# First weight matrix in two halves, squared half by half, and a first projection that begins with its high-times-high products

## The chip, the cores and the metric

The kernel runs on one core of one Trainium2 chip. The time is that of the device, in microseconds (us), for one execution. Five engines run their own instruction streams in parallel and meet at semaphores: TensorE (PE in the profile, its weight loads PEld), VectorE (DVE), ScalarE (ACT), GpSimd (POOL) and SyncE (SP), which here only issues transfers.

## The reference

One transformer-like layer on x of shape (4, 512, 512): a gated recurrent mixer, then a feed-forward part with a Walsh-Hadamard transform.

```python
def mixer(h, Wi, Wf, Wg, Wo, gnorm_w):          # h = layernorm(x)
    i = einsum('bth,dh->btd', h, Wi)
    f = einsum('bth,dh->btd', h, Wf)
    g = einsum('bth,dh->btd', h, Wg)
    gate = sigmoid(f)
    v = silu(i) * (1.0 - gate)
    o = scan over t of  o[t] = gate[t] * o[t-1] + v[t]
    rms = o * rsqrt(mean(o * o) + 1e-5)
    return einsum('btd,hd->bth', rms * gnorm_w * g * sigmoid(g), Wo)

def ffn(z, W1, W2, W3):                         # z = layernorm(x1)
    hidden = fwht(silu(z @ W1.T) * (z @ W3.T))
    return hidden @ W2.T

x1  = x  + layernorm(mixer(layernorm(x), ...))
out = x1 + layernorm(ffn(layernorm(x1), ...))
```

## The kernel before

The four batches b are worked one after the other, overlapped. Each has 4 row tiles t of 128 rows. Every fp32 operand of a product is split into two fp16 parts, high and low, and a product is made of three TensorE passes: high times high (L615), high times low (L616) and low times high (L617), into one PSUM bank.

The order of the work on each engine is written out in tables (PE_ORDER, ACT_ORDER, DVE_ORDER, POOL_ORDER, SP_ORDER). Each engine runs its table from front to back, and each step waits on semaphores for its inputs. A step is named KIND.b.t; on TensorE a number behind a colon is the PSUM bank. The steps at the start of the program are:

- X1.0.t (DVE L1072 to L1080): statistics of row tile t of batch 0. GpSimd then takes the power -1/2 (L1393).
- X2.0.t (DVE L1085): normalises tile t.
- XT.0.t on PE (L667): four 128x128 fp32 transposes of tile t. XT.0.t on ACT (L866) writes the high part to xb, XT.0.t on DVE (L1094) the low part.
- AQ.w.0 on ACT (L877): squares the whole attention matrix w (0 is W_f, 1 W_i, 2 W_g), 2048 elements in each partition. AQ.3.0 does W_o in two parts (L874).
- AN.w.0 on PE (L689): four matmuls of ones by the squares, a sum over partitions. AN.w.0 on DVE (L1100 and six small ones) makes the scale row_s of the matrix from it.
- AT.w.c on ACT (L881) and on DVE (L1115): the high and the low part of column chunk c of matrix w.
- F.0.c, I.0.c, G.0.c on PE: the projections with W_f, W_i and W_g, 12 matmuls of 512 columns each.
- W2N.m.0 on PE (L760): eight products of unit m of the raw second feed-forward weight with itself, which wait for the load of that unit (w2t).

F.0.0 waits for all four high and all four low parts of x, and for the low part of chunk 0 of W_f:

```python
pe.wait_ge(xt_hi, TC * (b + 1))
pe.wait_ge(xt_lo, TC * (b + 1))
...
pe.wait_ge(aw_lo[w], c + 1)          # in project()
```

All loads go through one queue, issued by SyncE in this order: row tile 0, the identity (eye, for the transposes), row tiles 1 to 3, W_f, W_i, W_g, gnorm, W_o; the row tiles of batch 1, each after the transpose of the tile of batch 0 that it replaces; the Hadamard matrix, eight pairs of W_1 and W_3, four units of W_2, and so on.

Of the kernel before, what the change touches and what calls it, by code (L numbers as in the profile page):

```python
# [42 lines left out]
GA.0.4:6 H2.0.1:0 H2.1.0:2 UP.0.4:5 GA.0.5:7 UP.0.5:3 GA.0.6:1 UP.0.6:6 H2.1.1:5 GA.0.7:7 UP.0.7:3 H2.2.0:1
H2.2.1:6 GA.0.8:4 UP.0.8:0 GA.0.9:7 UP.0.9:3 H2.3.0:2 MS.1.0:4 H2.3.1:5 GA.0.10:1 UP.0.10:0 Y.1.0:7 Y.1.1:1
H2.4.0:4 H2.4.1:3 GA.0.11:6 H2.5.0:2 H2.5.1:0 UP.0.11:5 GA.0.12:6 UP.0.12:7 GA.0.13:5 Y.1.2:6 Y.1.3:1 H2.6.0:7
H2.6.1:4 H2.7.0:3 UP.0.13:2 GA.0.14:0 UP.0.14:6 GA.0.15:5 UP.0.15:7 H2.7.1:2 D.0.0 D.0.1 D.0.2 D.0.3 D.0.4 D.0.5
D.0.6 D.0.7 D.0.8 D.0.9 D.0.10 D.0.11 D.0.12 D.0.13 D.0.14 D.0.15 D.0.16 D.0.17 D.0.18 D.0.19 D.0.20 D.0.21
# [37 lines left out]
AQ.0.0 XT.0.0 XT.0.1 XT.0.2 AQ.1.0 XT.0.3 AT.0.0 AT.0.1 AT.0.2 AQ.2.0 AT.0.3 AT.1.0 AT.1.1 AT.1.2 AQ.3.0 F.0.0  # L85
AT.1.3 AT.2.0 AT.2.1 I.0.0 WN.0.0 AT.2.2 XT.1.0 F.0.1 WN.1.0 AT.3.0 G.0.0 WN.2.0 I.0.1 AT.2.3 S.0.0 P.0.0 XT.1.1
F.0.2 XT.1.2 I.0.2 AT.3.1 G.0.1 S.0.1 XT.1.3 AT.3.2 P.0.1 AT.3.3 F.0.3 G.0.2 I.0.3 S.0.2 F.1.0 P.0.2 WN.3.0
S.0.3 G.0.3 P.0.3 F.1.1 I.1.0 G.1.0 WN.4.0 WN.5.0 I.1.1 WN.6.0 WN.7.0 S.1.0 YN.0.0 YN.0.1 YN.0.2 YN.0.3 WT.0.0
WT.0.1 WT.1.0 WT.1.1 ZT.0.0 WT.2.0 F.1.2 P.1.0 F.1.3 WT.2.1 G.1.1 S.1.1 ZT.0.1 ZT.0.2 ZT.0.3 I.1.2 GA.0.0 P.1.1
# [1404 lines left out]
```

## Time and profile before

| | us |
|---|---|
| median of 3 runs (692.3 to 694.3) | 692.82 |
| the profiled execution | 692.09 |
| its span on the core | 690.3 |
| PE busy | 668.9 (97%) |
| DVE busy | 484.3 (70%) |
| ACT busy | 285.4 (41%) |

The span runs from the first to the last instruction that the profile shows; the profiled execution's own time is 1.8 us longer. The idle time of TensorE is in few places: 8.95 us ahead of its first instruction, and the waits that are listed below. The granted clock of TensorE is shown by stretch as PEclk, 1.00 being 2.4 GHz and 0.50 being 1.2 GHz. A busy time of the matmuls is modelled, so the distance between starts is the better measure of their pace.

### The profile page before, as it was taken

Reading aid. Unit: us, or ns where it says so; the run is one execution under the profiler, and the core shown is the slowest. Engines: PE = TensorE matmul, PEld = TensorE weight load, DVE = VectorE, ACT = ScalarE, POOL = GpSimd, SP = SyncE. Lnnn points to the kernel's source line nnn. Section 1 sums busy time; section 2 is a strip of 40 time slices with the busy share of each in tenths; the row PEclk is TensorE's granted clock in tenths of the full one; section 3 lists DMA queues with packets and bytes.
Section 4 is the critical chain, followed back from the end, with each engine's and each line's share of the span. In section 5 each row is a group of like instructions: output and inputs, shape, how many; then the busy total and the mean of one; then the engine's idle time right before and its main releaser. Section 6 shows DMA issues by size and latency. Waiting matters only on the chain.

```text
span 690.3 us, 10939 instructions
## 1 busy us (share of the span) xinstructions
PE 668.9 (97%) x4132; PEld 407.3 (59%) x4132; DVE 484.3 (70%) x837; ACT 285.4 (41%) x466; POOL 266.5 (39%) x228
## 2 busy tenths in 40 slices
PE   3999999999998999999999999999999999999996
PEld 2545454444443454557877675656666777877762
DVE  6998999998988867976757461717478465744544
ACT  5978565764434325633322231452323221412231
POOL 1299479759254211552522211133256120311221
PEclk9999999999999999999999999999999999999999
DMA  8960421333569986385449336203526933432502
GB/s 340 406 237 24 160 77 51 132 97 117 184 218 297 235 241 226 140 335 181 152 155 275 140 64 227 101 21 123 182 93 173 252 126 122 138 129 101 198 1 92
DMA packets 58820, 113.30 MB, mean 164 GB/s; under 512 B 33424, under 2 KB 37776, under 8 KB 54160
## 3 DMA queue, kind: packets, MB, share of 16 engines
...
q8 instruction: 33, 0.54, 0.3%
q14 instruction: 19, 0.16, 0.1%
...
## 4 chain that ended last, share of the span: by engine, by line
PE 90%; DMA 4%; DVE 2%; issue 1%; SPq 1%; POOL 1%; ACT 0%; DVEq 0%; POOLq 0%
PE ps L615 29%; PE ps L616 29%; PE ps L617 29%; DMA w2t<-W2t 2%; PE ps L775 2%; PE ps L667 1%; DMA ring<-W13t 1%; DMA rows<-L_attn_hidden_states 1%; SPq L522 1%; PE ps L726 1%; PE ps L760 0%; POOL rstd L1393 0%; DVE ring L1278 0%; DVE w2t L1342 0%; DVE sg L1168 0%
## 5 line engine op out<-in xcount | busy, mean ns | idle before, releaser
L615 PE MATMUL ps<-xb,ring 128*128 128x256 f16 (+1 forms) x704 | 225.9, 321 | 1.1 <-DVE ring L1115 1.0
L617 PE MATMUL ps<-xb,ring 128*128 128x256 f16 (+1 forms) x704 | 225.9, 321 | 0.0
L616 PE MATMUL ps<-xb,ring 128*128 128x256 f16 (+1 forms) x704 | 225.9, 321 | 0.0
L615 PEld LDWEIGHTS ps<-xb,ring 128*128 128x128 f16 x704 | 69.1, 98 | 48.0 <-issue 3.3
L616 PEld LDWEIGHTS ps<-xb,ring 128*128 128x128 f16 x704 | 68.9, 98 | 46.7 <-issue 2.7
L1393 POOL TENSOR_TENSOR rstd<-var,neg_half 128x1 f32<-128x1 f32 x64 | 46.0, 723 | 125.3 <-DVE var L1080 38.5
L617 PEld LDWEIGHTS ps<-xb,ring 128*128 128x128 f16 x704 | 68.8, 98 | 42.1
L1450 POOL TENSOR_TENSOR ring<-sga,ring 128x512 f16<-128x512 f32 x36 | 47.8, 1334 | 117.3 <-ACT ring L1029 117.3
L616 PE MATMUL ps<-ring 128*128 128x256 f16 x288 | 78.5, 273 | 0.0
L617 PE MATMUL ps<-ring 128*128 128x256 f16 x288 | 78.5, 273 | 0.0
L615 PE MATMUL ps<-ring 128*128 128x256 f16 x288 | 78.5, 273 | 0.0
L1292 DVE TENSOR_TENSOR ring<-ps,junk 128x512 f32<-128x512 f32 x48 | 32.9, 687 | 55.5 <-ACT sga L1017 25.1
L1450 POOL TENSOR_TENSOR hsp<-sga,hsp 128x512 f16<-128x512 f32 x24 | 29.0, 1216 | 82.1 <-ACT hsp L1029 82.1
L1302 DVE TENSOR_TENSOR ring<-ps,ring 128x512 f32<-128x512 f32 x48 | 33.0, 687 | 34.4 <-PE ps L617 33.1
L996 ACT ACTIVATE junk<-ps 128x256 f32<-128x256 f32 x48 | 18.1, 380 | 91.8 <-PE ps L617 87.0
L615 PE MATMUL ps<-w2t,ring 128*128 128x512 f16 x144 | 54.6, 379 | 0.0
L616 PE MATMUL ps<-w2t,ring 128*128 128x512 f16 x144 | 54.6, 379 | 0.0
L617 PE MATMUL ps<-w2t,ring 128*128 128x512 f16 x144 | 54.6, 379 | 0.0
L1313 DVE TENSOR_TENSOR ring<-ps,ring 128x512 f32<-128x512 f32 x48 | 32.8, 686 | 28.8 <-PE ps L617 28.7
L1362 DVE SCALAR_TENSOR_TENSOR sga<-ring,up_c,sga 128x512 f32<-128x512 f32 x48 | 38.2, 808 | 13.3 <-ACT sga L1017 12.9
L1017 ACT ACTIVATE sga<-ring,gate_c 128x512 f32<-128x512 f32 x48 | 33.8, 716 | 29.0 <-DVE ring L1313 11.6
L1029 ACT ACTIVATE ring<-sga 128x512 f16<-128x512 f32 x36 | 22.0, 624 | 46.0 <-DVE sga L1362 28.3
...
## 6 DMA issues: line engine op xcount, KB each, us to landing
...
```

What stands on the lines that cost most here:

```text
L615: pe.matmul(dst, a_hi, b_hi, start=start, stop=False)
L616: pe.matmul(dst, a_hi, b_lo, start=False, stop=False)
L617: return pe.matmul(dst, a_lo, b_hi, start=False, stop=stop)
L996: act.activation(p_copy[:, g % 2], bank("GP", b, g)[:, 256:512], ACT.Copy).then_inc(sp_rdy, 1)
L1017: act.activation(sga[:, c % 2], src, ACT.Silu, scale=gate_c[:]).then_inc(sga_rdy, 1)
L1029: act.activation(hid(b, c, 0), sga[:, c % 2], ACT.Copy).then_inc(hid_hi, 1)
L1292: dve.tensor_tensor(combined(g % 2)[:, 0:512].rearrange("p (o t) -> p o t", o=2), bank("GQ", b, g)[:].rearrange("p (o t) -> p o t", o=2), ...
L1302: dve.tensor_tensor(to[:, 512:1024].rearrange("p (o t) -> p o t", o=2), bank("GR", b, g)[:].rearrange("p (o t) -> p o t", o=2), both, ALU. ...
L1313: dve.tensor_tensor(to[:, 512:1024], bank("GU", b, g)[:], to[:, 512:1024], ALU.add).then_inc(gu_rdy, 1)
L1362: dve.scalar_tensor_tensor(sga[:, c % 2], src, up_c[:], sga[:, c % 2], ALU.mult, ALU.mult).then_inc(hid_rdy, 1)
L1393: pool.tensor_tensor(dst, src, neg_half[:].broadcast_to(src.shape), ALU.pow).then_inc(done, 1)
L1450: pool.tensor_tensor(hid(b, c, 1), sga[:, c % 2], hid(b, c, 0), ALU.subtract).then_inc(hid_lo, 1)
```

## The change

W_f comes in two transfers of 512 KB, one issued behind row tile 0, ahead of the identity, and one behind row tile 1. Each half is squared on its own, AQ.0.0 and AQ.0.1. On ACT, AQ.0.1 stands behind XT.0.0, and AQ.1.0 (the squares of W_i) goes from ahead of XT.0.3 to behind AT.0.0. On PE, AN.0.0 goes ahead of XT.0.3, and waits between its second and third matmul for the second half. On DVE, X1.0.2 goes behind X2.0.1, and AN.0.0 goes from behind XT.0.2 to ahead of XT.0.0. F.0.0 makes the same 12 products in another order, four high times high, four high times low and four low times high, with a wait ahead of each group. The five tables are otherwise what they were; they are laid out anew, so of each only its head is shown.

```diff
 PE_ORDER = """
-XT.0.0:4 XT.0.1:5 XT.0.2:6 XT.0.3:7 AN.0.0:0 AN.1.0:1 F.0.0:2 AN.2.0:3 ...
+XT.0.0:4 XT.0.1:5 XT.0.2:6 AN.0.0:0 XT.0.3:7 AN.1.0:1 F.0.0:2 AN.2.0:3 ...
 ACT_ORDER = """
-AQ.0.0 XT.0.0 XT.0.1 XT.0.2 AQ.1.0 XT.0.3 AT.0.0 AT.0.1 AT.0.2 AQ.2.0 ...
+AQ.0.0 XT.0.0 AQ.0.1 XT.0.1 XT.0.2 XT.0.3 AT.0.0 AQ.1.0 AT.0.1 AT.0.2 AQ.2.0 ...
 DVE_ORDER = """
-X1.0.0 X1.0.1 X1.0.2 X2.0.0 X2.0.1 X1.0.3 X2.0.2 X2.0.3 XT.0.0 XT.0.1 XT.0.2 AN.0.0 XT.0.3 ...
+X1.0.0 X1.0.1 X2.0.0 X2.0.1 X1.0.2 X1.0.3 X2.0.2 X2.0.3 AN.0.0 XT.0.0 XT.0.1 XT.0.2 XT.0.3 ...
...
             load_x(0, 0)
+            sp.dma_start(att_raw(0)[:, 0:2], w_f[:, 0:2]).then_inc(ld_aw[0], 16)
             sp.dma_start(ident[:], eye).then_inc(ld_eye, 16)
             load_x(0, 1)
+            sp.dma_start(att_raw(0)[:, 2:4], w_f[:, 2:4]).then_inc(ld_wf, 16)
             load_x(0, 2)
             load_x(0, 3)
-            load_attention(0, w_f)
...
-                pe.wait_ge(aw_sq, w + 1)
+                pe.wait_ge(aw_sq, 1 if w == 0 else w + 2)
...
                 for k in range(KC):
+                    if w == 0 and k == 2:
+                        pe.wait_ge(aw_sq, 2)
...
             def f(b, c):
+                if b == 0 and c == 0:
+                    wait_bank("F", 0, 0)
+                    pe.wait_ge(xt_hi, TC)
+                    pe.wait_ge(aw_hi[0], 1)
+                    w, dst = att_w(0), bank("F", 0, 0)[:]
+                    for k in range(KC):
+                        pe.matmul(dst, w[:, 0, k, chunk(0)], xb[:, 0, 0, k, :], start=k == 0, stop=False)
+                    pe.wait_ge(xt_lo, TC)
+                    for k in range(KC):
+                        pe.matmul(dst, w[:, 0, k, chunk(0)], xb[:, 0, 1, k, :], start=False, stop=False)
+                    pe.wait_ge(aw_lo[0], 1)
+                    for k in range(KC):
+                        last = pe.matmul(dst, w[:, 1, k, chunk(0)], xb[:, 0, 0, k, :], start=False, stop=k == KC - 1)
+                    last.then_inc(f_mm, 1)
+                    return
...
             def square_attention(w, p):
+                if w == 0:
+                    act.wait_ge(ld_wf if p else ld_aw[0], 16)
+                    half = slice(1024 * p, 1024 * (p + 1))
+                    act.activation(squares[0][:, half], att_raw(0).rearrange("p k d -> p (k d)")[:, half], ACT.Square
+                                   ).then_inc(aw_sq, 1)
+                    return
                 act.wait_ge(ld_aw[w], 16)
```

On TensorE at the start of the program, before: the last transposes of x, the sums of squares of W_f (bank ps0) and W_i (ps1), and the first products of F.0.0 (ps2).

```order
L667 MATMUL ps6<-ident,rows 128x128 [waits x_norm]
L667 MATMUL ps6<-ident,rows 128x128 x3
L667 MATMUL ps7<-ident,rows 128x128 [waits x_norm]
L667 MATMUL ps7<-ident,rows 128x128 x3
L689 MATMUL ps0<-ot,ones16 128x512 [waits ones16_set,aw_sq]
L689 MATMUL ps0<-ot,ones16 128x512 x3
L689 MATMUL ps1<-ot,ones16 128x512 [waits aw_sq]
L689 MATMUL ps1<-ot,ones16 128x512 x3
L615 MATMUL ps2<-xb,ring 128x512 [waits aw_lo0,xt_lo,xt_hi]
```

The same place on TensorE in the changed kernel:

```order
L663 MATMUL ps6<-ident,rows 128x128 x3
L687 MATMUL ps0<-ot,ones16 128x512 [waits ones16_set,aw_sq]
L687 MATMUL ps0<-ot,ones16 128x512
L687 MATMUL ps0<-ot,ones16 128x512 [waits aw_sq]
L687 MATMUL ps0<-ot,ones16 128x512
L663 MATMUL ps7<-ident,rows 128x128 [waits x_norm]
L663 MATMUL ps7<-ident,rows 128x128 x3
L687 MATMUL ps1<-ot,ones16 128x512 [waits aw_sq]
L687 MATMUL ps1<-ot,ones16 128x512 x3
L713 MATMUL ps2<-xb,ring 128x512 [waits aw_hi0,xt_hi]
L713 MATMUL ps2<-xb,ring 128x512 x3
L716 MATMUL ps2<-xb,ring 128x512 [waits xt_lo]
```

The sums of W_f now stand ahead of the transposes of tile 3 (ps7). Those of W_i (ps1) still stand ahead of F.0.0 (ps2).

On ScalarE at the start, before: the squares of W_f, the high parts of tiles 0 to 2, the squares of W_i (the second row with ot and 2048), the high part of tile 3, and the first high parts of W_f.

```order
L877 ACTIVATE ot<-ring 128x2048 [waits ld_aw0]
L866 ACTIVATE xb<-ps4 128x4x128 [waits xt_mm]
L866 ACTIVATE xb<-ps5 128x4x128 [waits xt_mm]
L866 ACTIVATE xb<-ps6 128x4x128 [waits xt_mm]
L877 ACTIVATE ot<-ring 128x2048 [waits ld_aw1]
L866 ACTIVATE xb<-ps7 128x4x128 [waits xt_mm]
L881 ACTIVATE ring<-ring,row_s 128x4x128 [waits aw_srdy] x3
```

The same place on ScalarE in the changed kernel:

```order
L885 ACTIVATE ot<-ring 128x1024 [waits ld_aw0]
L879 ACTIVATE xb<-ps4 128x4x128 [waits xt_mm]
L885 ACTIVATE ot<-ring 128x1024 [waits ld_wf_second]
L879 ACTIVATE xb<-ps5 128x4x128 [waits xt_mm]
L879 ACTIVATE xb<-ps6 128x4x128 [waits xt_mm]
L879 ACTIVATE xb<-ps7 128x4x128 [waits xt_mm]
L900 ACTIVATE ring<-ring,row_s 128x4x128 [waits aw_srdy]
L896 ACTIVATE ot<-ring 128x2048 [waits ld_aw1]
L900 ACTIVATE ring<-ring,row_s 128x4x128 [waits aw_srdy] x2
```

The squares of W_i (L896, ot, 2048) now stand behind the high part of tile 3 and behind the first high part of W_f.

## Rows read from the trace of the kernel before

**Rows 1.** Waits of TensorE over the whole span: us in total, times, longest.

```profile
PE ps L667 <- DVE rows L1085: 9.0, 1, 9.0
PE ps L615 <- DVE w2t L1342: 2.4, 1, 2.4
PE ps L689 <- ACT ot L877: 1.5, 1, 1.5
...
PE ps L615 <- DVE ring L1115: 1.0, 1, 1.0
```

**Rows 2.** Timeline, TensorE, 8.9 to 17.3: start, us, what, idle before and releaser.

```profile
8.95 3.90 PE L667 MATMUL ps<-ident,rows 128*128 128x128 f32 x16 [8.95 <-DVE rows L1085]
12.68 1.03 PE L689 MATMUL ps<-ot,ones 128*128 128x512 bf16 x4
15.17 1.04 PE L689 MATMUL ps<-ot,ones 128*128 128x512 bf16 x4 [1.46 <-ACT ot L877]
17.17 0.38 PE L615 MATMUL ps<-xb,ring 128*128 128x512 f16 x1 [0.96 <-DVE ring L1115]
```

**Rows 3.** Timeline, TensorE, 32 to 34, the products with W2.

```profile
32.30 0.62 PE L760 MATMUL ps<-w2t 128*128 128x128 bf16 x8
33.22 0.63 PE L760 MATMUL ps<-w2t 128*128 128x128 bf16 x8 [0.30 <-DMA w2t<-W2t]
```

**Rows 4.** Chain of waits, 0 to 50: start, us, what.

```profile
18.02 15.15 DMA w2t<-W2t
```

**Rows 5.** Busy time by stretch: PE, PEld, DVE, ACT, POOL, then clock, DMA share, GB/s.

```profile
0.00:5.00 5.00, 0.00 (x0) 0.00 (x0) 1.43 (x7) 1.49 (x2) 0.50 (x5) 1.00 0.59 177
5.00:6.00 1.00, 0.00 (x0) 0.00 (x0) 0.00 (x0) 0.00 (x0) 0.26 (x1) 1.00 1.10 381
16.00:33.00 17.00, 15.96 (x85) 8.14 (x84) 15.62 (x45) 16.87 (x27) 3.65 (x4) 1.00 1.03 405
```

**Rows 6.** Timeline, VectorE, 6 to 15.

```profile
6.17 0.69 DVE L1072 BATCH_NORM_STATS2 st<-rows 128x6 f32<-128x512 f32 x1 [1.61 <-DMA rows<-L_attn_hidden_states]
...
7.22 0.68 DVE L1072 BATCH_NORM_STATS2 st<-rows 128x6 f32<-128x512 f32 x1
...
8.27 0.99 DVE L1085 TENSOR_SCALAR rows<-rows,mv,rstd 128x512 f32<-128x512 f32 x2
9.18 0.69 DVE L1072 BATCH_NORM_STATS2 st<-rows 128x6 f32<-128x512 f32 x1
...
11.20 0.55 DVE L1085 TENSOR_SCALAR rows<-rows,mv,rstd 128x512 f32<-128x512 f32 x1 [0.44 <-POOL rstd L1393]
...
14.18 0.68 DVE L1100 TENSOR_REDUCE exps<-ps 128x1 f32<-128x512 f32 x1
```

**Rows 7.** Timeline, ScalarE, 9 to 20.

```profile
9.94 1.91 ACT L877 ACTIVATE ot<-ring 128x2048 bf16<-128x2048 f32 x1 [7.72 <-DMA ring<-L_attn_Wf]
...
13.19 1.92 ACT L877 ACTIVATE ot<-ring 128x2048 bf16<-128x2048 f32 x1
14.99 0.61 ACT L866 ACTIVATE xb<-ps 128x512 f16<-128x512 f32 x1
15.52 1.95 ACT L881 ACTIVATE ring<-ring,row_s 128x512 f16<-128x512 f32 x3
17.37 1.90 ACT L877 ACTIVATE sga<-ring 128x2048 bf16<-128x2048 f32 x1
19.17 2.54 ACT L881 ACTIVATE ring<-ring,row_s 128x512 f16<-128x512 f32 x4
```

**Rows 8.** Timeline, TensorE, around the first down projection.

```profile
207.05 1.02 PE L775 MATMUL ps<-w2t,had 128*128 128x512 f32 x2
210.50 0.51 PE L615 MATMUL ps<-w2t,hsp 128*128 128x512 f16 x1 [2.42 <-DVE w2t L1342]
```

**Rows 9.** Busy time by stretch, around the first down projection.

```profile
208.00:210.50 2.50, 0.07 (x1) 0.03 (x1) 1.67 (x3) 2.30 (x4) 0.00 (x0) 1.00 0.93 277
210.50:214.00 3.50, 3.50 (x9) 1.31 (x10) 3.40 (x7) 0.34 (x1) 0.00 (x0) 0.52 1.02 344
```

More of the change, by code:

```diff
@@ L43 @@
[L43 to L47, printed above, removed]
@@ new lines @@
+AN.3.0:1 GC.0.0:3 G.0.0:2 W2N.0.0:5 W2N.1.0 I.0.2:4 F.0.2:3 G.0.1:1 G.0.2:2 XT.1.2:6 I.0.3:7 G.0.3:3 XT.1.3:0 F.0.3:4
+W2N.2.0 F.1.0:1 F.1.1:6 G.1.0:0 I.1.0:4 I.1.1:2 W2N.3.0 MS.0.0:7 Y.0.0:1 Y.0.1:3 Y.0.2:6 Y.0.3:4 F.1.2:0 F.1.3:7
+WS.0.0:2 G.1.1:1 G.1.2:3 ZT.0.0:6 W2N.4.0 W2N.5.0 I.1.2:2 G.1.3:4 ZT.0.1:0 ZT.0.2:7 W2N.6.0 W2N.7.0 ZT.0.3:1 I.1.3:6
+GA.0.0:0 W2S.0.0:5 UP.0.0:7 GA.0.1:2 UP.0.1:1 GA.0.2:0 UP.0.2:5 GA.0.3:2 H2.0.0:7 UP.0.3:1 GA.0.4:6 H2.0.1:0 H2.1.0:2
+UP.0.4:5 GA.0.5:7 UP.0.5:3 GA.0.6:1 UP.0.6:6 H2.1.1:5 GA.0.7:7 UP.0.7:3 H2.2.0:1 H2.2.1:6 GA.0.8:4 UP.0.8:0 GA.0.9:7
@@ new lines @@
+GR.1.7:5 GU.1.7:7 D.1.10 D.1.11 GQ.1.8:6 GR.1.8:5 D.1.12 D.1.13 GU.1.8:4 D.1.14 D.1.15 GP.1.9:7 GQ.1.9:6 GR.1.9:5
+GP.1.10:7 D.1.16 GQ.1.10:6 GU.1.9:5 D.1.17 D.1.18 GR.1.10:7 GP.1.11:4 D.1.19 D.1.20 D.1.21 GQ.1.11:5 D.1.22 D.1.23
+D.1.24 D.1.25 GR.1.11:4 GP.1.12:6 GU.1.10:7 GQ.1.12:5 D.1.26 D.1.27 GP.1.13:4 GU.1.11:7 D.1.28 GR.1.12:6 GU.1.12:5
+D.1.29 D.1.30 GP.1.14:4 GQ.1.13:7 GQ.1.14:6 GR.1.13:4 GP.1.15:7 D.1.31 D.1.32 GQ.1.15:4 GU.1.13:5 D.1.33 D.1.34
+GR.1.14:5 D.1.35 GU.1.14:6 D.1.36 D.1.37 D.1.38 D.1.39 D.1.40 D.1.41 D.1.42 GP.2.0:7 GQ.2.0:5 GP.2.1:6 GR.1.15:4
@@ new lines @@
+GQ.2.1:7 GU.1.15:6 D.1.43 D.1.44 D.1.45 D.1.46 GR.2.0:5 D.1.47 D.1.48 GR.2.1:4 D.1.49 GU.2.0:6 GP.2.2:5 GU.2.1:7
+GP.2.3:4 D.1.50 D.1.51 D.1.52 D.1.53 GQ.2.2:5 D.1.54 D.1.55 D.1.56 D.1.57 F.3.0:6 D.1.58 GR.2.2:4 D.1.59 G.3.0:7
+I.3.0:5 GU.2.2:4 F.3.1:7 D.1.60 D.1.61 D.1.62 GQ.2.3:5 GR.2.3:6 GP.2.4:7 GP.2.5:5 D.1.63 GU.2.3:6 I.3.1:7 G.3.1:5
+GQ.2.4:4 GP.2.6:6 F.3.2:7 I.3.2:5 D.2.0 G.3.2:7 GR.2.4:5 GP.2.7:4 D.2.1 F.3.3:6 D.2.2 GQ.2.5:5 GU.2.4:7 D.2.3 GQ.2.6:6
+GR.2.5:7 GR.2.6:5 I.3.3:4 GU.2.5:7 GU.2.6:6 D.2.4 GP.2.8:5 GP.2.9:7 D.2.5 D.2.6 D.2.7 D.2.8 G.3.3:5 D.2.9 D.2.10
@@ new lines @@
+GQ.2.7:4 D.2.11 D.2.12 D.2.13 D.2.14 GR.2.7:6 GU.2.7:5 MS.3.0:4 GP.2.10:7 GQ.2.8:6 D.2.15 D.2.16 D.2.17 D.2.18 GR.2.8:6
+Y.3.0:7 Y.3.1:6 Y.3.2:5 D.2.19 GU.2.8:4 Y.3.3:7 GQ.2.9:6 GR.2.9:4 D.2.20 GQ.2.10:5 D.2.21 GU.2.9:6 GP.2.11:7 D.2.22
+D.2.23 GP.2.12:4 D.2.24 D.2.25 GQ.2.11:6 D.2.26 D.2.27 D.2.28 GR.2.10:5 D.2.29 GP.2.13:7 GU.2.10:4 GQ.2.12:5 GR.2.11:6
+GR.2.12:7 D.2.30 D.2.31 D.2.32 D.2.33 D.2.34 D.2.35 GP.2.14:4 GP.2.15:5 GU.2.11:6 D.2.36 GU.2.12:7 D.2.37 GQ.2.13:4
+D.2.38 GQ.2.14:6 GR.2.13:7 GU.2.13:4 D.2.39 D.2.40 D.2.41 D.2.42 D.2.43 D.2.44 GR.2.14:5 GU.2.14:6 D.2.45 D.2.46
@@ L82 @@
+D.3.59 D.3.63
 """
 ACT_ORDER = """
[L85 to L89, printed above, removed]
@@ new lines @@
+ZT.0.0 WT.2.0 F.1.2 P.1.0 F.1.3 WT.2.1 G.1.1 S.1.1 ZT.0.1 ZT.0.2 ZT.0.3 I.1.2 GA.0.0 P.1.1 WT.3.0 WT.3.1 WT.4.0 GA.0.1
+UP.0.0 I.1.3 WT.4.1 WT.5.0 UP.0.1 WT.5.1 WT.6.0 S.1.2 WT.6.1 WT.7.0 WT.7.1 GA.0.2 GA.0.3 H2.0.0 UP.0.2 G.1.2 WT.8.0
+WT.8.1 WT.9.0 WT.9.1 WT.10.0 GA.0.4 UP.0.3 WT.10.1 WT.11.0 WT.11.1 GA.0.5 UP.0.4 UP.0.5 GA.0.6 WT.12.0 H2.0.1 P.1.2
+H2.1.0 WT.12.1 G.1.3 WT.13.0 WT.13.1 GA.0.7 WT.14.0 P.1.3 UP.0.6 H2.1.1 H2.2.0 UP.0.7 S.1.3 WT.14.1 GA.0.8 GA.0.9
+UP.0.8 H2.2.1 H2.3.0 WT.15.0 GA.0.10 UP.0.9 WT.15.1 H2.3.1 SH.0.0 H2.4.0 GA.0.11 UP.0.10 YN.1.0 GA.0.12 YN.1.1 SH.1.0
@@ new lines @@
+GP.1.8 ZT.2.4 GA.1.6 GA.1.7 GP.1.9 ZT.2.5 UP.1.6 ZT.2.6 UP.1.7 GP.1.10 GP.1.11 GA.1.8 GA.1.9 UP.1.8 UP.1.9 GA.1.10
+GA.1.11 GP.1.12 GP.1.13 GP.1.14 UP.1.10 UP.1.11 XT.3.0 XT.3.1 GA.1.12 GA.1.13 XT.3.2 GP.1.15 UP.1.12 GP.2.0 GA.1.14
+GP.2.1 UP.1.13 GA.1.15 UP.1.14 XT.3.3 GP.2.2 GA.2.0 UP.1.15 GP.2.3 GA.2.1 G.3.0 UP.2.0 I.3.0 F.3.0 S.3.0 F.3.1 GA.2.2
+GP.2.4 W.1.0 UP.2.1 W.1.1 GP.2.5 I.3.1 UP.2.2 P.3.0 G.3.1 W.1.2 F.3.2 I.3.2 GA.2.3 GP.2.6 P.3.1 G.3.2 GA.2.4 F.3.3
+S.3.1 W.1.3 UP.2.3 GP.2.7 GA.2.5 GP.2.8 S.3.2 I.3.3 P.3.2 S.3.3 G.3.3 UP.2.4 GP.2.9 UP.2.5 GA.2.6 P.3.3 GA.2.7 UP.2.6
@@ new lines @@
+GP.2.10 UP.2.7 YN.3.0 YN.3.1 YN.3.2 YN.3.3 GA.2.8 GA.2.9 ZT.3.0 GP.2.11 GP.2.12 UP.2.8 UP.2.9 ZT.3.1 ZT.3.2 GP.2.13
+ZT.3.3 ZT.3.4 GA.2.10 GA.2.11 ZT.3.5 ZT.3.6 UP.2.10 GP.2.14 UP.2.11 GA.2.12 GA.2.13 GP.2.15 UP.2.12 UP.2.13 GP.3.0
+GA.2.14 GA.2.15 UP.2.14 UP.2.15 GA.3.0 GA.3.1 GP.3.1 GP.3.2 GP.3.3 UP.3.0 GP.3.4 W.2.0 GA.3.2 UP.3.1 GP.3.5 W.2.1
+GA.3.3 GP.3.6 W.2.2 UP.3.2 UP.3.3 W.2.3 GP.3.7 GA.3.4 GA.3.5 GP.3.8 GP.3.9 UP.3.4 UP.3.5 GA.3.6 GA.3.7 GP.3.10 GP.3.11
+UP.3.6 UP.3.7 GA.3.8 GA.3.9 GP.3.12 UP.3.8 UP.3.9 GP.3.13 GA.3.10 GA.3.11 UP.3.10 UP.3.11 GP.3.14 GP.3.15 GA.3.12
@@ new lines @@
+WT.4.0 WT.4.1 WT.5.0 WT.5.1 WT.6.0 WT.6.1 UP.0.2 WT.7.0 H2.0.0 WT.7.1 UP.0.3 WT.8.0 WT.8.1 WT.9.0 WT.9.1 P.1.2 WT.10.0
+UP.0.4 WT.10.1 S.1.3 UP.0.5 WT.11.0 WT.11.1 FD.5.0 FD.5.1 UP.0.6 FD.5.2 H2.0.1 P.1.3 WT.12.0 WT.12.1 WT.13.0 WT.13.1
+FD.5.3 WT.14.0 UP.0.7 FD.5.4 FD.5.5 H2.1.0 H2.1.1 H2.2.0 FD.5.6 UP.0.8 FD.5.7 SA.0.0 MS.1.0 UP.0.9 WT.14.1 H2.2.1
+WT.15.0 H2.3.0 Y.1.0 UP.0.10 SO.0.0 H2.3.1 Y.1.1 FD.7.0 FD.7.1 YN.1.0 YN.1.1 FD.7.2 FD.7.3 WT.15.1 UP.0.11 FD.7.4
+SA.1.0 UP.0.12 FD.7.5 H2.4.0 FD.7.6 SO.1.0 H2.4.1 FD.7.7 Y.1.2 H2.5.0 H2.5.1 Y.1.3 SA.2.0 YN.1.2 Z1.1.0 YN.1.3 H2.6.0
@@ new lines @@
+GR.2.2 S.3.0 V.1.0 UP.2.1 GQ.2.3 GR.2.3 V.1.1 UP.2.2 W.1.0 GU.2.2 GU.2.3 V.1.2 P.3.0 S.3.1 V.1.3 GQ.2.4 P.3.1 GR.2.4
+GU.2.4 UP.2.3 GQ.2.5 GR.2.5 GQ.2.6 GR.2.6 GU.2.5 S.3.2 P.3.2 UP.2.4 GU.2.6 S.3.3 UP.2.5 GQ.2.7 W.1.1 P.3.3 GR.2.7
+UP.2.6 W.1.2 GQ.2.8 GR.2.8 GU.2.7 MS.3.0 Y.3.0 UP.2.7 Y.3.1 YN.3.0 YN.3.1 Y.3.2 Z1.3.0 GU.2.8 W.1.3 YN.3.2 Y.3.3 GQ.2.9
+YN.3.3 Z2.3.0 GR.2.9 UP.2.8 GU.2.9 Z1.3.1 UP.2.9 GQ.2.10 Z1.3.2 Z1.3.3 Z2.3.1 Z2.3.2 Z2.3.3 ZT.3.0 GR.2.10 GQ.2.11
+GU.2.10 ZT.3.1 ZT.3.2 ZT.3.3 GQ.2.12 ZT.3.4 GR.2.11 GR.2.12 UP.2.10 ZT.3.5 ZT.3.6 GU.2.11 GU.2.12 UP.2.11 GQ.2.13
@@ L149 @@
+GU.3.14 GU.3.15 UP.3.14 UP.3.15 V.3.0 V.3.1 W.3.0 W.3.1 V.3.2 V.3.3 W.3.2 W.3.3
 """
```

148 lines of the change are left out of this document (53 added, 95 removed).

## The prediction

> **What bounds the kernel now.** I read the busy shares first: TensorE is busy for 97% of the span, so a change pays only if it moves TensorE's own instructions. The waits of TensorE come next [rows 1]. The longest, 9.0 us, ends with the first normalised row tile; 1.5 and 1.0 us more lie between the squares and the first projection; 2.4 us stand ahead of the first down projection. Third comes the timeline at the start [rows 2]. Sixteen transposes run from 8.95 on, 3.90 us or 0.24 us each; the four sums of W_f start at 12.68 and those of W_i at 15.17, after 1.46 us of idling for ScalarE; F.0.0 starts at 17.17, after 0.96 us for VectorE's low part. From there TensorE has no gap up to 32.30, where the products with raw W_2 begin, and it then waits 0.30 us for a load of W_2 [rows 3]. The chain of waits follows that load back for 15.15 us to its issue at 18.02 [rows 4]: the queue has long been full, and 405 GB/s over 16 to 33 us [rows 5] is what it moves.
>
> So there are two limits side by side in the first 33 us: TensorE's own path, and the queue, which is only 0.3 us behind it. Whatever TensorE gains ahead of 33.2 it gives back at that wait. Whatever it loses beyond 0.3 us goes on, since it has no gap behind it up to the wait of 2.42 us at 210.50 [rows 8], which ends a short path of its own: a TensorE product with the Hadamard matrix at 207.05, then ScalarE, then VectorE, then TensorE again. That path moves with TensorE and takes up nothing.
>
> **The loads.** The same bytes go through the same queue. Row tile 1 now has 512 KB of W_f ahead of it that it didn't have. At 405 GB/s these 0.524 MB take 1.29 us. Before, VectorE began on tile 1 at 6.17, right when it landed [rows 6]; now that is at about 7.5. The other bound: the queue had moved 5 x 177 GB/s = 0.885 MB by 5 us and moves 381 GB/s then [rows 5], and tile 0, half of W_f, the identity and tile 1 are 1.114 MB, so they could all be there at 5.6 if no share of the tile lags behind the mean as it did before. I take 7.5, from the nearest row, and keep 5.6 for the range. The second half of W_f lands 1.3 us after tile 1, tile 3 at 10.1.
>
> The Trainium skill, DMA: Bandwidth & Descriptors, section "Measured (HBM→SBUF, 128 partitions, SWDGE, issued from GpSimd)", asks for at least 1 MiB in one transfer to reach 78% of the peak, 341 GB/s, and speaks against the halves. The stretch from 16 to 33 us is fed mostly with transfers of 512 KB and holds 405 GB/s [rows 5], so the trace doesn't bear the rule out with a full queue. By the page W_f would take 3.1 us instead of 2.6, an estimate, and tile 3 would land 0.5 us later, which has slack.
>
> **The row tiles.** VectorE takes a tile's statistics in 1.05 us (7.22 to 8.27) and normalises it in 0.5 (half of 0.99). From the start of a tile's statistics to the start of its normalisation, with GpSimd's power between, it is 2.02 us (9.18 to 11.20) [rows 6]. In the new order: tile 1's statistics 7.5, tile 0 normalised 8.55 to 9.1, tile 1 9.5 to 10.0, statistics of tile 2 at 10.0 and of tile 3 at 11.05, tile 2 normalised 12.1 to 12.65, tile 3 from 13.1 to 13.6. TensorE starts 0.68 us after a normalisation starts (8.27 to 8.95), so the first transpose is at 9.2, the third tile's at 12.75, and 1.6 us of idling stands between them, which the old order didn't have.
>
> **The scale of W_f.** At full pace the third tile's transposes take 0.5 us (half of 4 x 0.24), the four sums, now ahead of tile 3, 0.86 (four at 0.215), to 14.1. The squares of the second half are ready: ScalarE begins them after the high part of tile 0, at about 10.8, and half of 1.91 us [rows 7] is 1. VectorE reads the sums at 14.25 at once, where before they waited for its low parts until 14.18; ScalarE's first AT of W_f starts 1.34 us after that read (14.18 to 15.52) [rows 6, 7], now at 15.6. So the new order of the sums gives back nothing: the later tiles have used it up. If the transposes and sums still run at half pace, it is 1.4 us later, 17.0: TensorE's first stretch took 3.7 us of unbroken work before its pace doubled at 12.6 [rows 2], and now it is broken.
>
> **F.0.0, the step that decides.** Its first four products no longer wait for the low parts. But the sums of W_i stand ahead of it on TensorE, in both kernels, and the squares of W_i now stand on ScalarE behind AT.0.0. They were from 13.19 to 15.11, beside the transposes, and cost F.0.0 nothing. Now they run after AT.0.0: 15.6 + 0.62 (a third of 1.85, 15.52 to 17.37) + 1.92 = 18.15 [rows 7], the sums until 19.05, and F.0.0 starts at about 19.05 against 17.17: 1.9 us late. The low parts that it was to run ahead of are done by then: VectorE makes the scale until 15.8, four low parts at 0.63 (a third of 1.89) until 18.3, the low part of W_f by 19.05. The splitting of F.0.0 into three groups costs nothing, 12 products as before, and gives nothing. ScalarE is full from 15 to 33 (16.87 of 17.00 [rows 5]). Between the first AT and AT.0.3 it has 3.65 us of work before (15.52 to 19.17) and 1.80 more now, since the squares of W_i came in; so it is late by the same 1.9 us, and VectorE, which reads from it, by about as much. I.0.0 and G.0.0 follow F.0.0 with the same distances and wait for nothing new.
>
> The Trainium skill, TensorE: Matmul & The Clock Gate, section "Step-by-step: what each phase is for", says that only weight loads are pulled ahead and matmuls stay in program order. By it F.0.0 can't pass the waiting sums. No row of before has such a case; what passing would give is a rival below.
>
> **The clock.** Between the transposes of tile 3 (until 14.6) and the sums of W_i (18.2) TensorE now idles 3.6 us, at least 3.1 in every variant: high part of tile 3 0.53, AT.0.0 0.62, squares 1.92. At 210.5, after an idle of 2.42 us, its granted clock was 0.52 in the next 3.5 us, the level of 1.2 GHz, and 1.00 before it [rows 8, 9]. After 1.46 and 0.96 us at 15.17 and 17.17 it stayed at full pace [rows 2]. So I take a fall here, and its price from the rows at that level: 3.4 us at half pace, 1.7 us lost. Bounds: 0 if it stays, 2.6 if the low stretch is longer by half.
>
> **Sum.** 1.9 (F.0.0) + 1.7 (clock) - 0.3 (the wait for W_2 that closes) = 3.3 us. SyncE is moved too: its loads behind row tile 0 of batch 1 wait for the transposes of x and are issued up to 2 us later, but the queue has some 5 us of work before it by then (the load issued at 18.02 waited 15.15), which hides it. Against the profiled execution, 692.09, that gives 695.4. That execution is 0.7 us under the median of 692.82, which I leave as noise.
>
> **Rivals.**
> 1. The clock doesn't fall. For it: the first gaps didn't lower it. Against it: this gap is longer than the one at 208. 1.9 - 0.3 = +1.6, or about 0 if tile 1 lands at 5.6: 692.1 to 693.7.
> 2. The change does what it says: F.0.0 starts ahead of the squares of W_i, from the high parts at 16.3. That needs TensorE to pass the sums of W_i. The 0.9 us gained end at the load of W_2 that lands at 33.2: 692.1, no change.
> 3. Faster. One mechanism, at the first down projection: there the clock falls after an idle of 2.42 us only, and a shifted start may leave it up, which gives back 1.7 us (half of 3.4). It decides only if tile 1 also lands near 5.6 and the early loss is near 0: 690.3. With the full loss it only cuts the sum to 1.6.
> 4. Slower still: the transposes and sums stay at half pace, +1.4, and the low stretch is the long one, 2.6: 3.3 + 1.4 + 0.9 = 5.6, 697.7.
>
> **How the numbers follow.** Forecast 0.54, rival 1 0.26, rival 2 0.07, rival 3 0.06, rival 4 0.07. A measurement of this kernel tells about 0.3% from no change, 2.1 us, so the bounds lie at 690.7 and 694.9 about 692.8. Some of the forecast's case (tile 1 early by a part of its 1.9 us) falls under 694.9: slower 0.60. Rivals 1 and 2 and that part: same 0.33. Faster 0.07. The forecast's own range is 693.8 to 697.3. The range for 8 in 10 takes in rival 1 and most of rival 4: 692.0 to 697.9.
>
> **What would show it.** In the timeline after: statistics of tile 1 at 7.5; the sums of W_f ahead of tile 3's transposes at about 13.3; TensorE idle for over 3 us with ScalarE's squares of W_i as the releaser; F.0.0 at about 19; a granted clock under 1 from 18 to 22; and no wait for W_2 at 33, with its first products at about 36. I am wrong if F.0.0 starts at or under 17.2, if tile 1's statistics start at 6, or if TensorE's products with W_2 begin by 33.

## The result, and the profile after

| | before | changed |
|---|---|---|
| median, us (9 runs each) | 692.82 (692.3 to 694.3) | 695.93 (694.87 to 697.68) |
| ratio to before, 95% interval | | 1.0041 (1.0029 to 1.0053) |
| profiled execution, us | 692.09 | 695.85 |
| its span, us | 690.3 | 694.1 |

The changed kernel is slower: 0.41% of 692.8 is 2.8 us, with an interval of 2.0 to 3.7. The two medians are 3.1 us apart and the two profiled executions 3.8; the prediction said 3.3.

The waits of TensorE after (us in total, times, longest), against [rows 1]:

```profile
PE ps L663 <- DVE rows L1104: 10.0, 2, 8.5
PE ps L687 <- ACT ot L896: 3.2, 1, 3.2
PE ps L611 <- DVE w2t L1361: 2.4, 1, 2.4
PE ps L739 <- DVE ring L1324: 1.4, 1, 1.4
```

The wait of 1.5 us for ScalarE's squares of W_i is now 3.2 us, the row tiles have a second wait, and the 1.0 us for VectorE ahead of F.0.0 and the 0.3 us for the load of W_2 are gone. The timeline of TensorE at the start, against [rows 2]:

```profile
8.54 2.02 PE L663 MATMUL ps<-ident,rows 128*128 128x128 f32 x8 [8.54 <-DVE rows L1104]
11.99 1.12 PE L663 MATMUL ps<-ident,rows 128*128 128x128 f32 x4 [1.43 <-DVE rows L1104]
12.90 1.91 PE L687 MATMUL ps<-ot,ones 128*128 128x512 bf16 x4
14.60 0.98 PE L663 MATMUL ps<-ident,rows 128*128 128x128 f32 x4
18.78 1.89 PE L687 MATMUL ps<-ot,ones 128*128 128x512 bf16 x4 [3.19 <-ACT ot L896]
20.46 1.89 PE L713 MATMUL ps<-xb,ring 128*128 128x512 f16 x4
22.16 1.05 PE L716 MATMUL ps<-xb,ring 128*128 128x512 f16 x4
23.05 1.03 PE L719 MATMUL ps<-xb,ring 128*128 128x512 f16 x4
```

F.0.0 (L713, L716, L719) starts at 20.46 instead of 17.17. The sums of W_i ahead of it (18.78) and its first four products take 1.7 us each, 0.42 us for a matmul; the next four start 0.22 us apart (22.16 to 23.05). ScalarE at the same time, against [rows 7]:

```profile
10.16 1.05 ACT L885 ACTIVATE ot<-ring 128x1024 bf16<-128x1024 f32 x1
...
15.62 0.60 ACT L879 ACTIVATE xb<-ps 128x512 f16<-128x512 f32 x1 [1.88 <-PE ps L663]
16.20 0.72 ACT L900 ACTIVATE ring<-ring,row_s 128x512 f16<-128x512 f32 x1
16.83 1.89 ACT L896 ACTIVATE ot<-ring 128x2048 bf16<-128x2048 f32 x1
18.63 1.32 ACT L900 ACTIVATE ring<-ring,row_s 128x512 f16<-128x512 f32 x2
```

High part of tile 3, AT.0.0, squares of W_i: these three fill TensorE's idle time from 15.6 to 18.8 one after the other. VectorE, against [rows 6]:

```profile
6.80 0.70 DVE L1091 BATCH_NORM_STATS2 st<-rows 128x6 f32<-128x512 f32 x1 [2.24 <-DMA rows<-L_attn_hidden_states]
...
14.85 0.69 DVE L1119 TENSOR_REDUCE exps<-ps 128x1 f32<-128x512 f32 x1 [1.93 <-PE ps L687]
...
16.33 2.47 DVE L1113 TENSOR_TENSOR xb<-ps,xb 128x512 f16<-128x512 f32 x4
18.72 1.41 DVE L1134 SCALAR_TENSOR_TENSOR ring<-ring,row_s 128x512 f16<-128x512 f32 x2
```

Tile 1's statistics start at 6.80 (6.17 before), and VectorE idles 1.93 us for the sums of W_f, with the four low parts of x waiting behind them. The first products with W_2, against [rows 3], and the down projection, against [rows 8]:

```profile
36.46 1.08 PE L773 MATMUL ps<-w2t 128*128 128x128 bf16 x16
...
214.29 0.38 PE L611 MATMUL ps<-w2t,hsp 128*128 128x512 f16 x1 [2.43 <-DVE w2t L1361]
```

All sixteen products with W_2 run in one go, 4.16 us later than before, with no wait for the load. From there TensorE has no new wait above 0.2 us, and the down projection is 3.79 us later than before. By stretch, with the columns of [rows 5, 9]:

```profile
18.80:22.20 3.40, 3.40 (x9) 1.19 (x10) 2.63 (x10) 3.40 (x4) 0.00 (x0) 0.50 1.01 393
...
214.00:218.00 4.00, 3.71 (x18) 1.74 (x19) 3.90 (x8) 0.76 (x2) 0.00 (x0) 1.00 0.95 335
298.70:302.10 3.40, 3.40 (x9) 1.20 (x10) 2.48 (x5) 1.98 (x3) 0.00 (x0) 0.50 1.00 426
```

The granted clock is 0.50 (1.2 GHz) from 18.8 to 22.2. At the down projection it didn't fall in this execution, though the wait is the same; it fell after the 1.4 us wait of L739 (row sums, at 297.5) instead. Before, it was the other way round [rows 9], so these two cancel between the two profiles.

### The profile page after: what moved, and what is told of

Its sections match the earlier page's. It is cut to its first block, busy times and chain, and to the rows that moved or that the text cites. A ratio compares the mean times of both kernels' runs of the same rounds, so it can differ in the third digit from the quotient of the medians.

```text
span 694.1 us, 10941 instructions
## 1 busy us (share of the span) xinstructions
PE 671.1 (97%) x4132; PEld 407.9 (59%) x4132; DVE 485.4 (70%) x837; ACT 285.8 (41%) x467; POOL 266.6 (38%) x228
## 4 chain that ended last, share of the span: by engine, by line
PE 92%; DVE 3%; DMA 2%; issue 1%; POOL 1%; ACT 1%; DVEq 0%; SPq 0%; POOLq 0%
PE ps L611 29%; PE ps L612 29%; PE ps L613 29%; PE ps L788 2%; DMA ring<-W13t 1%; PE ps L663 1%; DMA rows<-L_attn_hidden_states 1%; PE ps L687 1%; POOL rstd L1412 1%; PE ps L773 1%; PE ps L739 0%; DVE ring L1297 0%; DVE w2t L1361 0%; DVEq L1092 0%; ACT ot L896 0%
```

## The experiments

The ratios are to the kernel before, run on the same chip beside each (one chip for experiments 1 to 8, another for 9 and 10); their intervals reach 0.0013 to 0.0019 to either side. The mean granted clock of an execution, named at some places, is that over its whole span, 1.00 being full speed throughout. In the timelines F.0.0 and the first products with W_2 are the markers.

**1. The squares of W_i back in their place.**

```diff
 ACT_ORDER (changed kernel)
-... XT.0.1 XT.0.2 XT.0.3 AT.0.0 AQ.1.0 AT.0.1 ...
+... XT.0.1 XT.0.2 AQ.1.0 XT.0.3 AT.0.0 AT.0.1 ...
```

> The changed kernel with one step put back: the squares of W_i stand on ScalarE ahead of the high part of tile 3, as before the change; all else is as changed. Theory (the squares of W_i behind AT.0.0 hold the sums of W_i, and these hold F.0.0; the gap lowers the clock): sums of W_i at about 15.6, F.0.0 at about 17.3 instead of 20.46, its last group done at about 20.4 since the low parts of x end at 18.7 on VectorE and the low part of W_f at 19.4; time 692.8 to 693.6. Rival (the cost is in the later row tiles and the loads): the time stays near 695.9, at most 1 us less.

Measured: 694.25, ratio 1.0013 (0.9997 to 1.0028). TensorE's timeline:

```profile
15.58 1.89 PE L687 MATMUL ps<-ot,ones 128*128 128x512 bf16 x4
17.26 1.28 PE L713 MATMUL ps<-xb,ring 128*128 128x512 f16 x4
18.85 1.04 PE L716 MATMUL ps<-xb,ring 128*128 128x512 f16 x4 [0.31 <-DVE xb L1113]
19.72 1.03 PE L719 MATMUL ps<-xb,ring 128*128 128x512 f16 x4
```

The sums of W_i and F.0.0 come where the theory had them, 3.2 us earlier than in the changed kernel, and the 3.19 us of idling are gone. Its ratio is lower by 0.0028, 1.9 us. So this one step makes most of the loss. The time stays some 0.9 us over the kernel before, a bit above the expected span, though the interval takes in 1, no difference. TensorE has 1.9 us of waits for VectorE that neither kernel has: 0.31 at 18.85, 0.28 at 24.48, 0.41 at 49.56, and the longest for a row tile of batch 1:

```profile
28.59 0.63 PE L663 MATMUL ps<-ident,rows 128*128 128x128 f32 x4 [0.92 <-DVE rows L1104]
```

Experiment 9 takes that up.

**2. Only the squares of W_i moved, in the kernel before.**

```diff
 ACT_ORDER (kernel before)
-... XT.0.2 AQ.1.0 XT.0.3 AT.0.0 AT.0.1 ...
+... XT.0.2 XT.0.3 AT.0.0 AQ.1.0 AT.0.1 ...
```

> The kernel before with that one step alone moved: the squares of W_i stand on ScalarE behind AT.0.0, W_f is loaded and squared whole. Theory: scale of W_f at 15.5 as before, squares 16.1 to 18.0, sums of W_i at 18.0 after 4.3 us of idling, F.0.0 at 18.9 or, with the clock down, 19.8; 1.8 us late and 1.7 us for the clock, less 0.5 at the load of W_2: 695.8. Rival (loads and row tiles): 692.8, no change, since these are as before.

Measured: 695.76, ratio 1.0040 (1.0027 to 1.0053).

```profile
17.80 1.33 PE L689 MATMUL ps<-ot,ones 128*128 128x512 bf16 x4 [4.79 <-ACT ot L877]
18.93 0.63 PE L615 MATMUL ps<-xb,ring 128*128 128x512 f16 x1
```

The wait is 4.8 us, F.0.0 starts at 18.93, and its first six matmuls and a part of the seventh run at half clock. This step alone, with loads, halves and row tiles as before, costs what the whole change costs (1.0040 against 1.0041). Here the clock's part shows over the runs too: the mean granted clock is 0.9910 in its 12 runs against 0.9938 in the 29 of the kernel before, and 0.0028 of 690 us is 1.9 us, about what one stretch of 3.4 us at half clock loses (1.7). The rival that puts the loss on the loads is out as the main cause.

**3. The gap filled.** The changed kernel with matmuls that nobody reads, between the transposes of tile 3 and the sums of W_i.

```diff
+                if w == 1:
+                    for _ in range(15):
+                        pe.matmul(bank("AN", 2, 0)[:], ones16[:], squares[0][:, 0:D], start=True, stop=True)
                 pe.wait_ge(aw_sq, 1 if w == 0 else w + 2)
```

> The changed kernel with 15 more matmuls of 512 columns on TensorE, ones by squares of W_f into a bank that nobody reads before it is written anew, between the transposes of tile 3 and the sums of W_i, where TensorE idles for 3.19 us. Theory (1.7 us of the loss is the half clock after the gap): granted clock 1.00 at F.0.0, which starts at about 19.6 instead of 20.46 and runs its first products at 0.215 us; time 1.7 us less than the changed kernel, 694.2. Rival (the clock costs nothing, since VectorE and ScalarE are behind anyway): 695.9.

Measured: 696.16 median, ratio 1.0026 (1.0012 to 1.0041); 5 of the 12 times lie at 692.9 to 694.7, the other 7 at 696.1 to 697.5.

```profile
15.06 4.00 PE L683 MATMUL ps<-ot,ones 128*128 128x512 bf16 x15
18.89 1.03 PE L690 MATMUL ps<-ot,ones 128*128 128x512 bf16 x4
19.75 1.03 PE L716 MATMUL ps<-xb,ring 128*128 128x512 f16 x4
20.62 1.03 PE L719 MATMUL ps<-xb,ring 128*128 128x512 f16 x4
...
34.88 1.08 PE L776 MATMUL ps<-w2t 128*128 128x128 bf16 x16
```

The sums and F.0.0 run at full pace. From the start of the sums of W_i to the first products with W_2 it is 15.99 us, against 17.68 in the changed kernel (18.78 to 36.46): the 1.7 us of the theory, in these two profiles.

The whole time doesn't show them. The median is that of the rival (695.9), no better than the changed kernel's; by the ratios the kernel is 0.0015 or 1.0 us better, with the intervals overlapping. In the profiled execution, whose span of 694.5 us is even 0.4 longer than that of the changed kernel, the clock fell at both later places, where it fell at one of them in the changed kernel, and that takes the 1.7 us back:

```profile
214.40:217.70 3.30, 3.30 (x10) 1.13 (x9) 3.12 (x8) 1.57 (x2) 0.02 (x1) 0.51 0.92 308
299.30:302.50 3.20, 3.20 (x10) 1.20 (x9) 2.27 (x5) 1.98 (x3) 0.00 (x0) 0.54 1.00 426
```

The mean granted clock of the executions says the same: 0.995 to 0.999 in the five short ones, 0.993 in the seven long ones. So the clock's price at this place is shown in the timeline, and that filling the gap makes the kernel faster is not shown.

**4. F.0.0 ahead of the sums of W_i.**

```diff
 PE_ORDER (changed kernel)
-... XT.0.3:7 AN.1.0:1 F.0.0:2 AN.2.0:3 ...
+... XT.0.3:7 F.0.0:2 AN.1.0:1 AN.2.0:3 ...
```

> The changed kernel with F.0.0 ahead of the sums of W_i on TensorE. Theory: F.0.0 starts at about 16.9 with the high parts, waits for the low parts until 18.8 and ends at 20.4; the squares of W_i and W_g are as late as in the changed kernel, so the sums of W_g come at 21.8 and F.0.1 at about 22.6 against 20.62 before: about 1.5 to 2 us over the kernel before, 694.3 to 694.8. Rival (the early start of F.0.0 is all that was missing): F.0.1 at about 20 and a time of 692 or less.

Measured: 697.32, ratio 1.0053 (1.0034 to 1.0072), the slowest of all.

```profile
16.81 1.02 PE L713 MATMUL ps<-xb,ring 128*128 128x512 f16 x4 [1.40 <-ACT ring L900]
18.60 1.64 PE L716 MATMUL ps<-xb,ring 128*128 128x512 f16 x4 [0.77 <-DVE xb L1113]
20.03 1.91 PE L719 MATMUL ps<-xb,ring 128*128 128x512 f16 x4
21.74 1.31 PE L687 MATMUL ps<-ot,ones 128*128 128x512 bf16 x4
...
27.55 0.38 PE L611 MATMUL ps<-xb,ring 128*128 128x512 f16 x1 [1.04 <-DVE ring L1134]
31.65 0.63 PE L663 MATMUL ps<-ident,rows 128*128 128x128 f32 x4 [0.91 <-DVE rows L1104]
```

F.0.0 starts at 16.81 as expected (this also shows that its high inputs are there early in the changed kernel, where it is held by the sums of W_i alone), but waits for the low parts, the clock falls in the middle of it after two short waits, and the sums of W_i at 21.74 make VectorE late, with 1.95 us of new waits at 27.55 and 31.65. The expectation had left out the clock and undercounted VectorE: F.0.1 starts at 23.75 instead of 22.6, and the time is 2.5 us above the expected span. That F.0.0 begins early is worth nothing while W_i and W_g lag.

**5. The loads alone.** The kernel before with the loads and the first VectorE steps of the change, and W_f still squared whole.

```diff
             load_x(0, 0)
+            sp.dma_start(att_raw(0)[:, 0:2], w_f[:, 0:2]).then_inc(ld_aw[0], 16)
...
             load_x(0, 1)
+            sp.dma_start(att_raw(0)[:, 2:4], w_f[:, 2:4]).then_inc(ld_wf, 16)
...
 DVE_ORDER
-X1.0.0 X1.0.1 X1.0.2 X2.0.0 X2.0.1 ...
+X1.0.0 X1.0.1 X2.0.0 X2.0.1 X1.0.2 ...
```

> The kernel before with the new order of the loads (W_f in two halves behind row tiles 0 and 1) and the statistics of tile 2 behind the normalisation of tile 1; W_f is squared whole, all other steps stand as before, F.0.0 is made as before. Theory: tile 1's statistics at 6.8 instead of 6.17, the row tiles' transposes end at about 14.1, the sums of W_f follow, scale at 16.3, F.0.0 at 18.0 to 18.8; less 0.5 at the load of W_2: 0.5 to 1.2 us over the kernel before, 693.6 to 694.3. Rival (the loads cost nothing, all is the squares of W_i): 693.1.

Measured: 694.41, ratio 1.0021 (1.0005 to 1.0038), 1.5 us over.

```profile
11.97 2.10 PE L669 MATMUL ps<-ident,rows 128*128 128x128 f32 x8 [1.43 <-DVE rows L1089]
13.86 2.74 PE L691 MATMUL ps<-ot,ones 128*128 128x512 bf16 x8
18.53 0.59 PE L617 MATMUL ps<-xb,ring 128*128 128x512 f16 x1 [1.92 <-DVE ring L1119]
```

The late row tiles alone delay F.0.0 by 1.4 us (the sums of W_f and W_i are still at half pace in part: the eight take 2.74 us, where four take 1.03 in [rows 2]), and a wait of 1.92 us then sufficed to lower the clock in this execution. So the loads do cost, and the costs don't add, since experiment 2 costs as much without them as the change does with them: in the changed kernel the squares of W_i are the later of two things.

**6 to 8 and 10. Other orders, to beat the kernel before.** Experiment 6 keeps a part of the change (squaring by halves, the sums of W_f ahead of tile 3, F.0.0 in three groups), with W_f behind the row tiles and the squares of W_i as before. It also moves the first products with W_2:

```diff
 (changed kernel)
+load_x(0, 0), eye, load_x(0, 1..3), first half of W_f, second half of W_f
-ACT  AQ.0.0 XT.0.0 AQ.0.1 XT.0.1 XT.0.2 XT.0.3 AT.0.0 AQ.1.0 ...
+ACT  AQ.0.0 AQ.0.1 XT.0.0 XT.0.1 XT.0.2 AQ.1.0 XT.0.3 AT.0.0 ...
-DVE  ... X2.0.3 AN.0.0 XT.0.0 XT.0.1 XT.0.2 XT.0.3
+DVE  ... X2.0.3 XT.0.0 XT.0.1 AN.0.0 XT.0.2 XT.0.3
-PE   ... W2N.0.0:5 W2N.1.0 I.0.2:4 ...
+PE   ... I.0.2:4 W2N.0.0:5 W2N.1.0 ...
```

> The changed kernel with the halves of W_f behind row tile 3, where W_f was; both halves squared first on ScalarE; the squares of W_i ahead of the high part of tile 3, as before; on VectorE the statistics as before and the scale of W_f between the low parts of tiles 1 and 2; the sums of W_f ahead of the transposes of tile 3 and F.0.0 in three groups, as changed. And the first products with W_2 stand behind I.0.2 on TensorE, so that their load (33.2) isn't waited for. Theory: transposes at 8.95 as before, sums of W_f at 11.8, scale at 14.5, F.0.0 at 15.5, F.0.1 at 19.4 against 20.62: 0.7 to 1.2 us under the kernel before, 692.2. Rival (VectorE is the limit behind F.0.0, and its order is hurt by the early scale): no gain, 693.1.

Measured: 692.6, ratio 0.9985 (0.9968 to 1.0003). F.0.0 starts at 16.60 (17.17 before), not 15.5, since the first half of W_f only landed at 9.69 and all of ScalarE's chain follows it. In the profile of experiment 8, which has the same start and where that half landed at 8.36, it is 15.43. A gain of 1 us is likely and not shown.

Experiment 7 is the kernel before with one swap that has nothing to do with the change, at the largest wait behind the start. H2.7.1 is the last product with the Hadamard matrix, UP.0.15 the last group of the up projection of batch 0, and D.0.0 the first of its down projection:

```diff
 PE_ORDER (kernel before)
-... GA.0.15:5 UP.0.15:7 H2.7.1:2 D.0.0 ...
+... GA.0.15:5 H2.7.1:2 UP.0.15:7 D.0.0 ...
```

> The kernel before with one swap on TensorE: the last product with the Hadamard matrix (at 207.05) stands ahead of the last UP of batch 0 instead of behind it. That is not of the change; it is on the wait of 2.42 us that ends at 210.50 and where the clock fell. Theory: ScalarE and VectorE do its parts beside the 2.6 us of UP, the wait goes, and the fall of the clock with it: 2.4 to 4.1 us under the kernel before. Rival (another input of the down projection, the hidden parts or VectorE's work that UP delays, takes the wait's place): less than 1 us.

Measured: 690.18, ratio 0.9958 (0.9941 to 0.9975), 2.9 us under the kernel before and the lowest median here.

```profile
204.85 1.02 PE L775 MATMUL ps<-w2t,had 128*128 128x512 f32 x2
209.85 0.38 PE L615 MATMUL ps<-w2t,hsp 128*128 128x512 f16 x1 [1.39 <-DVE w2t L1342]
```

The wait shrinks from 2.42 to 1.39 us and does not go, and in this execution the clock did not fall behind it. The gain is more than the 1.0 us of wait. The mean granted clock of its 10 runs is 0.9966, against 0.9941 in the 32 of the kernel before beside them; 0.0025 of 690 us is 1.7 us, an estimate of the clock's part, and with the wait it makes the 2.9 nearly whole.

> e6_halves_behind_tiles and e7_last_transform_earlier in one kernel. Theory: the gains add, 3 to 5 us under the kernel before. Rival: as for the two.

Experiment 8, both: 691.15, ratio 0.9963 (0.9945 to 0.9981), 2.6 us under. The gains don't add within what this measures, and the expected 3 to 5 us were not reached.

```profile
15.43 1.02 PE L713 MATMUL ps<-xb,ring 128*128 128x512 f16 x4 [0.16 <-ACT ring L900]
```

> The kernel before with two swaps on TensorE and nothing of the change: the last Hadamard product ahead of the last UP of batch 0 (as in e7_last_transform_earlier), and the first two products with raw W_2 behind I.0.2. Theory: the second swap takes away the wait of 0.3 to 0.5 us for the load of W_2: 0.3 us under e7_last_transform_earlier, some 3.3 us under the kernel before. Rival (the transforms on GpSimd, which wait for these products, come later and hold something else): no better or worse than e7_last_transform_earlier.

Experiment 10, both swaps on the kernel before: 691.88, ratio 0.9972 (0.9955 to 0.9988). The wait for the load of W_2 is gone. TensorE waits twice for VectorE's low parts of the attention weights (L1115), 1.7 us in total; the first is the 0.96 us ahead of F.0.0 that the kernel before has too, the second is new:

```profile
47.07 0.38 PE L615 MATMUL ps<-xb,ring 128*128 128x512 f16 x1 [0.71 <-DVE ring L1115]
```

The rival holds as far as this measures: no gain over experiment 7 shows, though the two ran on different chips and their intervals overlap.

**9. The low parts of x back as well.**

```diff
 DVE_ORDER (as in experiment 1)
-... X2.0.3 AN.0.0 XT.0.0 XT.0.1 XT.0.2 XT.0.3
+... X2.0.3 XT.0.0 XT.0.1 XT.0.2 AN.0.0 XT.0.3
```

> e1_squares_back (the changed kernel with the squares of W_i put back) with one more step put back: on VectorE the low parts of tiles 0 to 2 stand ahead of the scale of W_f, as before the change. VectorE idles 1.93 us ahead of the scale in e1_squares_back, so the low parts fit there. Theory (what is left of the loss there, 0.9 us by time, is VectorE running behind: low parts until 18.7, waits of TensorE for it of 0.3 at F.0.0 and 0.7 later): F.0.0's last group ends near 19.7 instead of 20.6, these waits go, the first products with W_2 come about 1 to 1.5 us earlier than there (34.68): 692.5 to 693.3, at the kernel before. Rival (the later row tiles set it): F.0.0 and the time as in e1_squares_back.

Measured: 693.34, ratio 1.0002 (0.9987 to 1.0018).

```profile
17.18 1.26 PE L713 MATMUL ps<-xb,ring 128*128 128x512 f16 x4
18.28 1.03 PE L716 MATMUL ps<-xb,ring 128*128 128x512 f16 x4
19.14 1.03 PE L719 MATMUL ps<-xb,ring 128*128 128x512 f16 x4
...
32.85 1.28 PE L773 MATMUL ps<-w2t 128*128 128x128 bf16 x16
```

The waits for VectorE are gone, the last group starts at 19.14 instead of 19.72, and the products with W_2 come at 32.85 instead of 34.68. By the ratios the time is 0.0011 or 0.8 us better than in experiment 1, measured on another chip and with overlapping intervals. With two of its steps put back, the changed kernel ties with the kernel before, halves, loads and all.

## Why the prediction was right

**The step that decides** is the one it named: the squares of W_i behind AT.0.0 on ScalarE, with the sums of W_i still ahead of F.0.0 on TensorE. Experiment 2 shows it from one side, experiment 1 from the other. The reason why it costs so much is that the old place, beside TensorE's transposes, was free. Rival 2 needed TensorE to pass the waiting sums, and it didn't: AT.0.0, the last of F.0.0's high inputs, was done at 16.9, and F.0.0 started at 20.46, behind the sums.

**Its size was off and the errors partly cancelled.** AT.0.0 started at 16.20; the prediction had 15.6. Tile 1 landed earlier than assumed (statistics at 6.80, not 7.5), which gave 0.7 us back. But the transposes of the third tile and the sums of W_f ran at half pace: 0.91 us (11.99 to 12.90) where it counted 0.5, and 1.70 us (12.90 to 14.60) where it counted 0.86. That is the +1.4 us that it gave to rival 4 only, come true nearly whole, with tile 1 early by half as much. The granted clock doesn't show this half pace:

```profile
12.90:14.60 1.70, 1.70 (x5) 0.69 (x4) 0.02 (x1) 0.60 (x1) 0.00 (x0) 1.00 1.03 420
```

At full pace F.0.0 would follow AT.0.0's start by 3.45 us as the prediction adds it up, at 19.65, 2.5 us late instead of 1.9. A part of the agreement is luck.

**The clock.** Of the rest, 20.46 - 19.65 = 0.8 is the sums of W_i at half pace, and F.0.0's first four matmuls lose 0.85 more: 1.7 us in all, the term as forecast, in the profiled execution. The idle time was 3.19 us against the bound of 3.1 "in every variant". Experiment 3 takes just these 1.7 us out of the timeline, and not visibly out of the time. That the term holds for the median as well isn't shown (see what stays open).

**The load of W_2.** It was to give back 0.3 us. TensorE arrives 4.16 us late there and leaves 3.69 us late (37.38 against 33.69 for the next product), so it gives back 0.47: with the wait of 0.30 go 0.17 us between the starts that the row doesn't count as idle. 2.5 + 1.7 - 0.5 = 3.7, against 3.8 measured between the spans, and 3.3 predicted.

**Nothing behind takes it up.** The changed kernel is 3.69 us late at 37.4, 3.79 at the down projection and 3.8 at the end: held. In between, at the row sums, it is 2.10 us late (297.50 against 295.40), since the kernel before has had its fall of the clock at the down projection by then; the changed kernel has its own right behind the row sums. That the two profiled executions have one fall each behind the start is luck.

**What it missed.** It took VectorE to be late by no more than F.0.0. In the changed kernel that holds, since TensorE is later still. But the order on VectorE (scale of W_f ahead of the low parts) is a second cost, hidden behind the first: experiments 1 and 9 differ by it alone, and the timeline has the products with W_2 1.8 us apart. By the ratios it is 0.8 us, which the intervals don't tell from nothing. The prediction said the new order of the sums "gives back nothing"; with VectorE's order that came with it, it costs.

**What stays open.** Over many runs the difference is 2.8 us with an interval of 2.0 to 3.7, and the trace's 3.8 lies above it. The granted clock tells a part of why. In the twelve profiled executions its mean is 0.998 or 0.999 where the clock fell at none of three places (start, down projection, row sums), 0.995 or 0.996 with one fall, 0.993 or 0.994 with two, and 0.991 with three. Of the 84 runs of the kernel before beside the experiments, 16 are at 0.991 or less, so by this count it falls at the start there too. Their mean is 0.9939, that of the 9 runs of the changed kernel 0.9947. So the runs don't show the changed kernel longer at the low granted clock, and the 1.7 us of the profile are not shown as a part of the 2.8. Without them the sum is 1.6 as forecast (rival 1) and 2.0 with the other terms as measured, at the lower end of the interval. That 3.3 came near 2.8 may be luck in this term.

Nor do the runs of the changed kernel follow the clock: its four slowest, 696.49 to 697.68, have a mean of 0.996, and the four at 0.993 and 0.994 took 694.87 to 695.93, the profiled one among them. The four are 1.4 us longer on average, where fewer falls would make them shorter. Something that the granted clock doesn't show costs them time. A half pace at a granted clock of 1.00, as in the row above, could; there is no trace of such an execution, and it isn't shown.
